# A decoder layer in float32 by split products: first units, phase borders and the last coupling factors rearranged

## The reference

```
combined = 0.7 * gf + 0.3 * coupling_net(out)        # 512 -> 512 -> 256 -> 128 -> 1, gelu, sigmoid
coupling = 0.1 + adaptive_range * (combined - 0.5) * 2.0
out = out + coupling * twist(out)                    # twist permutes the four channel quarters, with signs
```

## Time and profile before

| | us |
|---|---|
| median of 3 runs | 2162.09 (2159.74 to 2171.07) |
| profiled execution, its own time | 2165.26 |
| its span | 2163.2 |
| PE busy, share of span | 1814.4, 84% |
| DVE busy | 1488.3, 69% |
| ACT busy | 1256.2, 58% |
| POOL busy | 857.7, 40% |

### The profile page before, as it was taken

One profiled execution on the slowest core, in us unless ns is written; L12 is line 12 of the kernel. 1 busy time (PEld: TensorE's weight loads), 2 busy tenths in 40 slices (PEclk: granted clock), 3 DMA queues, 4 the chain that ended last, 5 costly groups with the idle time before them and its releaser, 6 DMA issues. The chain is left out here.

```text
span 2163.2 us, 29349 instructions
## 1 busy us (share of the span) xinstructions
PE 1814.4 (84%) x8616; PEld 1353.1 (63%) x8616; DVE 1488.3 (69%) x2913; ACT 1256.2 (58%) x2664; POOL 857.7 (40%) x774
## 2 busy tenths in 40 slices
PE   6588888888888888888875999999958999988873
PEld 5465655656566565665434888888846777776652
DVE  6667677676776767677535666666644788888776
ACT  3277777777867868777752222222224677666754
POOL 4467767676775857768501222222210000000000
PEclk9689999999999999999887999999978999999986
DMA  4132132222323123132215111111031111212111
GB/s 143 37 91 59 49 98 58 88 58 62 88 54 108 46 77 86 34 98 59 80 37 180 59 58 58 58 58 58 20 103 58 59 54 45 78 59 78 59 39 58
DMA packets 90197, 148.90 MB, mean 69 GB/s; under 512 B 16496, under 2 KB 19568, under 8 KB 90096
## 3 DMA queue, kind: packets, MB, share of 16 engines
q1 hardware_dynamic: 90096, 147.76, 22.3%
HBM read 63.82 MB, written 33.55 MB: 45 GB/s over the span
## 5 line engine op out<-in xcount | busy, mean ns | idle before, releaser
L479 DVE TENSOR_REDUCE a_neg_max<-a_max 128x1 fp32r<-128x512 f32 x512 | 342.0, 687 | 175.5 <-PE a_max L819 170.0
L713 ACT ACTIVATE a_probs<-a_exp 128x512 f32<-128x512 f32 x512 | 294.2, 605 | 206.8 <-PE a_exp L837 205.9
L692 ACT ACTIVATE a_max<-a_max,a_neg_max 128x512 f32<-128x512 f32 x512 | 346.9, 689 | 27.0 <-DVE a_neg_max L479 26.5
L819 PE MATMUL a_max<-a_stack 96*128 96x512 f32 x512 | 223.5, 461 | 101.6 <-ACT a_max L692 90.7
L819 PEld LDWEIGHTS a_max<-a_stack 96*128 96x128 f32 x512 | 100.3, 199 | 195.9 <-ACT a_max L692 156.4
L837 PE MATMUL a_exp<-a_stack 100*128 100x512 f32 x512 | 197.7, 427 | 25.2 <-ACT a_probs L713 21.9
L794 PE MATMUL a_t<-a_w_hi,a_zT_hi 128*128 128x384 f32 x512 | 187.8, 367 | 26.3 <-DVE a_v L444 13.3
L317 POOL TENSOR_TENSOR a_rstd<-a_rstd,a_minus_half 128x16 f32<-128x16 f32 x64 | 186.2, 2909 | 44.4 <-DVE a_rstd L463 41.6
L795 PE MATMUL a_t<-a_w_lo,a_zT_hi 128*128 128x384 f32 x512 | 181.7, 355 | 0.0
L796 PE MATMUL a_t<-a_w_hi,a_zT_lo 128*128 128x384 f32 x512 | 181.2, 354 | 0.0
L1158 POOL TENSOR_TENSOR r_part<-r_part 128x512 f32<-128x512 f32 x32 | 45.8, 1431 | 315.1 <-DVE r_part L1205 315.1
(11 more groups left out here) (249 smaller groups left out, 4884.5 us busy)
## 6 DMA issues: line engine op xcount, KB each, us to landing
a_stack<-a_nT_hi SPq DMA_DIRECT2D x512, 64.0 KB, 2.0
a_stack<-a_nT_lo SPq DMA_DIRECT2D x256, 64.0 KB, 2.0
a_z<-x SPq DMA_DIRECT2D x8, 1024.0 KB, 7.3
a_y<-x SPq DMA_DIRECT2D x8, 1024.0 KB, 5.4
x<-a_y SPq DMA_DIRECT2D x8, 1024.0 KB, 4.2
r_xn<-x SPq DMA_DIRECT2D x8, 1024.0 KB, 5.6
r_cn<-ctx SPq DMA_DIRECT2D x8, 1024.0 KB, 7.8
x<-r_xn SPq DMA_DIRECT2D x8, 1024.0 KB, 4.3
```

The source lines that it names most:

```text
L479: nc.vector.tensor_reduce(neg_max[:, t, ROW + h:ROW + h + 1].bitcast(F32R), bank_max[i % NB][:, :], AX_X, ALU.max, negate=True).then_inc(m ...
L692: nc.scalar.activation(bank_max[i % NB][:, :], bank_max[i % NB][:, :], ACT.Exp, bias=neg_max[:, t, ROW + h:ROW + h + 1], accum_out=sums[:, ...
L713: nc.scalar.activation(probs[:, kt % 2, h, :], bank_exp[i % 2][:, :], ACT.Exp).then_inc(exp_done, 1)
L819: mm(bank_max[i % NB][:, :], stack[0:ROW, par, h, t * P:(t + 1) * P], stack[0:ROW, par, HG + h, :], start=True, stop=True).then_inc(score_ ...
```

## The change

Four places change.

- First units. `x_stats` of sequence 1 stands between unit 0's two `head_mean`, its fourth tile ahead of `turn_low(0, 0)`, `x_final` ahead of `turn_low(0, 1)`. Unit 2's projection gets four banks of its own and stands ahead of all query scores: two tiles behind the transposition of unit 0's first side, one behind the second side, the last behind `nTlo_done` 1. All `save_qkv` of unit 2 stand ahead of `row_max`. SP regroups units 0 and 1 side by side (key side of all four heads first), each as soon as its side is there. The head statistics `head_var(1, 1)` stay behind the fourth `row_max`.
- First border. Retention's weights, x1 and context of its first batch are loaded within attention once all projections are done, into the dead `w_hi`, `w_lo`; they are split into dead buffers, four of six parts (1024 columns each) in slots 3, 5, 8, 10 of the last unit, two around the last additions; DVE also takes the statistics and normalises x there (`next_stats` in slot 2, `next_norm` in slot 9). PE does 36 of the 48 output projections in slots 3 to 14 of the last unit. x1 is stored in four parts. The `turns` and `decay` tables are still loaded in retention, now first.
- Second border. Batch 7 follows a list of its own, `R_LAST`, with entries for coupling: `c_stats` and `c_shift` (DVE, POOL), `c_norm` (ACT), `c_split` 0 to 8 (ACT high, DVE low). Its loads are issued once the last v is projected. Coupling starts with the transpositions.
- Coupling. The third cycle's coupling is not multiplied in on 512 columns: PE turns `coupling`, `alpha` and `beta` (12 transpositions in place of 8) and DVE multiplies on 4 columns (`take_scale`, 8 small instructions in place of 3). `sums`, `l3_out`, `y`, `y_moments`, `y_norm` and `normalise` 3 move in `STAGES`.

```diff
+            def regroup_side(U, par, s):
+                c = SIDES[s]
+                sp.wait_ge(nTlo_done, 2 * U + s + 1)
...
-            regroup(0, 0)
-            regroup(1, 1)
+            for U in range(2):
+                for s in range(2):
+                    regroup_side(U, U, s)
...
-            sp.wait_ge(y_sum, T * B)
-            sp.dma_start(rows(x1, B - 1), y[:, :, :]).then_inc(x1_out, 16)
-            sp.wait_ge(x1_out, 16 * B)
+            sp.wait_ge(qkv_done, T * G * B)
+            for m in (0, 2, 1):
+                sp.dma_start(ret.raw[m], w_next[("Wk", "Wq", "Wv")[m]].rearrange("(k p) n -> p k n", p=P)).then_inc(ret.load_w, 16)
+            sp.dma_start(ret.xn[:, 0], rows(x1, 0)).then_inc(ret.x_in[0], 16)
+            sp.dma_start(ret.cn[:, :, :], rows(ctx_in, 0)).then_inc(ret.c_in, 16)
+            for t in range(T):
+                sp.wait_ge(y_sum, T * (B - 1) + t + 1)
+                sp.dma_start(x1[B - 1, t * P:(t + 1) * P, :], y[:, t, :]).then_inc(x1_out, 16)
+            sp.wait_ge(x1_out, 16 * (B - 1) + 16 * T)
...
+            def next_lower(m, half):
+                raw, hi, lo = ret.split_part(m, half)
+                dve.wait_ge(ret.w_high, SPLITS.index((m, half)) + 1)
+                nc.vector.tensor_tensor(lo, raw, hi.bitcast(F32), ALU.subtract).then_inc(ret.w_low, 1)
...
+                    if left == 0 and i == R_STATS_AT:
+                        next_stats()
+                    if left == 0 and i == R_NORM_AT:
+                        next_norm()
+                    if left == 0 and i in SPLIT_AT:
+                        next_lower(*SPLITS[SPLIT_AT.index(i)])
...
-            for s in range(2):
-                head_mean(0, s)
+            head_mean(0, 0)
+            for t in range(3):
+                x_stats(1, t)
+            head_mean(0, 1)
...
+            x_stats(1, 3)
             turn_low(0, 0, bank_t[0])
             rotate(1, 0)
             head_mean(1, 0)
+            x_final(1)
...
-            for h in range(HG):
-                for t in range(T):
-                    row_max(0, T * h + t)
-                if h == 0:
+            for t in range(T):
+                save_qkv(2, 2, t, bank_2[t])
+            for i in range(T * HG):
+                row_max(0, i)
+                if i == 3:
                     head_var(1, 1, False)
-                save_qkv(2, 2, h, bank_t[h % 2])
-                x_stats(1, h)
-            x_final(1)
...
             attn_low(G * B - 1, G - 1)
+            next_lower(*SPLITS[-2])
             for t in range(T):
-                add_out(B - 1, t, bank_t[t % 2])
+                add_out(B - 1, t, bank_last[t])
+            next_lower(*SPLITS[-1])
...
+                    if left == 0 and OUT_PART_AT <= i < OUT_PART_AT + T * (G - 1):
+                        if i == OUT_PART_AT:
+                            pe.wait_ge(attnT_done, U)
+                            pe.wait_ge(summed, T * HG * (U + 1))
+                            pe.wait_ge(maxrow_saved, 2 * (U + 1))
+                            pe.wait_ge(nTlo_done, 2 * (U + 1))
+                        project_out_part(*divmod(i - OUT_PART_AT, G - 1))
...
+            pe.wait_ge(qkv_saved, T + 3)
+            turn_heads(0, 0, bank_t[0])
+            for t in range(3):
+                if t == 2:
+                    pe.wait_ge(qkv_saved, T + 4)
+                    turn_heads(0, 1, bank_t[1])
                 for k in range(K):
-                    project(2, 2, h, k, bank_t[h % 2])
+                    project(2, 2, t, k, bank_2[t])
+            pe.wait_ge(nTlo_done, 1)
+            for k in range(K):
+                project(2, 2, 3, k, bank_2[3])
+            for i in range(T * HG):
+                query_scores(0, 0, i)
...
-            pe.wait_ge(nTlo_done, 2 * G * B)
-            pe.wait_ge(inverse_saved, G * B)
             for t in range(T):
-                if t >= 2:
-                    pe.wait_ge(y_sum, T * (B - 1) + t - 1)
-                project_out(B - 1, t, bank_t[t % 2])
+                project_out_part(t, G - 1)
...
+R_LAST = [(name, arg) for name, age, arg in R_STAGES if age == "now"][:19] + [
+    ("scores", 0), ("v_out", 3), ("scores", 1), ("mask", 0), ("mask", 1), ("c_stats", 0), ("scores", 2), ("s_out", 0),
+    ("mask", 2), ("c_split", 0), ("s_out", 1), ("c_split", 1), ("scores", 3), ("c_shift", 0), ("s_out", 2),
+    ("c_split", 2), ("mask", 3), ("c_split", 3), ("weigh", 0), ("s_out", 3), ("weigh", 1), ("c_norm", 0), ("c_norm", 1),
+    ("add", 0), ("c_split", 4), ("c_norm", 2), ("c_norm", 3), ("add", 1), ("weigh", 2), ("c_split", 5), ("weigh", 3),
+    ("add", 2), ("c_split", 6), ("c_split", 7), ("c_split", 8), ("add", 3)]
...
+            sp.wait_ge(v_done, T * B)
+            sp.dma_start(cou.xn[:, :, :], rows(x2, 0)).then_inc(cou.x_in, 16)
...
+            for dst, src in loads_w:
+                sp.dma_start(dst, src).then_inc(cou.load, 16)
...
+            for dst, src in loads_small:
+                sp.dma_start(dst, src).then_inc(cou.load_small, 16)
             store(B - 1, 1)
+            sp.wait_ge(cou.load_small, 16 * len(loads_small))
...
+                dve.wait_ge(cou.split_high, i + 1)
+                nc.vector.scalar_tensor_tensor(lo, raw, sign, hi.bitcast(F32), ALU.mult, ALU.subtract).then_inc(cou.split_low, 1)
...
+                act.wait_ge(cou.load, 16 * 4)
+                nc.scalar.activation(hi, raw, ACT.Copy, scale=sign).then_inc(cou.split_high, 1)
...
-    ("first", "new", 0), ("l3", "run", 0), ("scale", "old", 0), ("first_out", "new", 0), ("first_low", "new", 0),
-    ("first", "new", 1), ("y_scale", "old", 0), ("y", "old", 0), ("l3_out", "run", 0), ("z", "run", 0),
+    ("first", "new", 0), ("l3", "run", 0), ("scale", "old", 0), ("first_out", "new", 0), ("l3_out", "run", 0),
+    ("first_low", "new", 0), ("first", "new", 1), ("y_scale", "old", 0), ("y", "old", 0), ("z", "run", 0),
...
-    ("normalise", "next", 3), ("mul", "run", (2, 3)), ("mix", "run", (2, 3)), ("mixed", "run", (2, 1)),
+    ("mul", "run", (2, 3)), ("mix", "run", (2, 3)), ("mixed", "run", (2, 1)),
...
-    ("mixed", "run", (2, 3)), ("l2", "run", (2, 3)), ("second_out", "new", 3), ("y", "old", 2), ("y", "old", 3),
-    ("y_moments", "old", 0), ("transpose", "next", 0), ("transpose", "next", 1), ("transpose", "next", 2),
-    ("l2_out", "run", 2), ("turned", "next", 0), ("l3", "run", 2), ("turned", "next", 1), ("y_shift", "old", 0),
-    ("l3_out", "run", 2), ("l2", "new", (0, 0)), ("l2", "new", (0, 1)), ("z", "run", 2), ("transpose", "next", 3),
-    ("turned", "next", 2), ("y_norm", "old", 0), ("turned", "next", 3), ("sums", "run", 0), ("couple", "run", 2),
-    ("l2", "new", (0, 2)), ("l2", "new", (0, 3)), ("l2_out", "new", 0), ("gate", "new", 2)]
+    ("mixed", "run", (2, 3)), ("l2", "run", (2, 3)), ("sums", "run", 0), ("second_out", "new", 3),
+    ("normalise", "next", 3), ("y", "old", 2),
+    ("transpose", "next", 0), ("transpose", "next", 1), ("transpose", "next", 2), ("l2_out", "run", 2), ("y", "old", 3),
+    ("l3", "run", 2), ("y_moments", "old", 0), ("l3_out", "run", 2), ("turned", "next", 0), ("turned", "next", 1),
+    ("y_shift", "old", 0), ("l2", "new", (0, 0)), ("l2", "new", (0, 1)), ("z", "run", 2), ("transpose", "next", 3),
+    ("turned", "next", 2), ("y_norm", "old", 0), ("y_norm", "old", 1), ("turned", "next", 3), ("tanh", "run", 2),
+    ("l2", "new", (0, 2)), ("l2", "new", (0, 3)), ("l2_out", "new", 0), ("gate", "new", 2),
+    ("y_norm", "old", 2), ("y_norm", "old", 3)]
+
...
-                nc.vector.tensor_tensor(part[:, :], coupling[:, :], beta[:, :], ALU.mult).then_inc(dve_step, 1)
...
-                nc.vector.tensor_tensor(coupling[:, :], coupling[:, :], alpha[:, :], ALU.mult).then_inc(dve_step, 1)
...
-                nc.vector.tensor_tensor(alpha[:, :], alpha[:, :], part[:, :], ALU.subtract)
-                nc.vector.tensor_tensor(beta[:, :], beta[:, :], coupling[:, :], ALU.add).then_inc(coupled, 1)
...
+                nc.vector.tensor_copy(turned_rows[:, :, :], by_token[:, :, :, 0]).then_inc(scale_done, 1)
+                dve.wait_ge(scale_done, b + 1)
+                third, first, second = (turned_rows[:, i, :] for i in range(3))
+                nc.vector.tensor_scalar(third, third, derived[:, 2:3], base[:, par:par + 1], ALU.mult, ALU.add).then_inc(dve_step, 1)
...
+                nc.vector.tensor_tensor(crossed[:, 0, :], third, second, ALU.mult)
+                nc.vector.tensor_tensor(crossed[:, 1, :], third, first, ALU.mult).then_inc(dve_step, 1)
+                dve.wait_ge(dve_step, steps.next())
+                nc.vector.scalar_tensor_tensor(scale[:, 0, :], crossed[:, 0, :], -1.0, first, ALU.mult, ALU.add).then_inc(dve_step, 1)
+                nc.vector.tensor_tensor(scale[:, 1, :], second, crossed[:, 1, :], ALU.add)
+                nc.vector.scalar_tensor_tensor(scale[:, 2, :], second, -1.0, crossed[:, 1, :], ALU.mult, ALU.subtract)
+                dve.wait_ge(dve_step, steps.next())
```

(7 more changed lines are left out.)

414 lines of the change are left out of this document (235 added, 179 removed).

## The result

The changed kernel takes 2097.91 us (median of 4 runs, 2091.10 to 2099.41), the kernel before beside it 2164.32 us (median of 4, 2159.74 to 2171.07): ratio 0.9684, interval 0.9659 to 0.9710. The profiled execution took 2096.84 us with a span of 2093.9 us, against 2165.3 and 2163.2. So 66 us by the medians and 69.3 us by the spans, where 79 were forecast; 2097.91 lies inside 2060 to 2110.

A forecast was written before the change was run, and what follows sets the result against it. It took PE, with DVE close behind, to bound coupling passes, and chains of transfers and small steps the start and borders. Terms -13 - 24 - 14 - 28 = -79 us gave 2083 us, range 2060 to 2110.

The forecast's parts named there:

- First units: Start of attention: projections and statistics moved into existing waits bring the loop's start earlier, -13 us (from -8 to -17).
- First border: Attention to retention: 20.8 us in place of 44.9 up to retention's first product, -24 us (from -15 to -28).
- Second border: Retention to coupling: last addition +7.4 us, first coupling product at 1618.8 instead of 1632.76, -14 us (from -8 to -18).
- Coupling: Coupling passes, their boundaries and the end: PE's waits go or shrink, -28 us (from -15 to -50).
- pass 8 and the end: End of coupling: waits of 2.3 and 1.5 us into and in pass 8 go, and 1.8 us net at the end.
- rival 3: Start of attention: POOL's rotation or unit 1's stack holds the loop, -2 in place of -13, 2094 us; chance 7%.
- The longer unit: Attention's last unit, with 36 output projections moved in, ends 3.3 us later; bounds 0 and +12 (low clock throughout).
- Rival 1: Whole kernel: thin cover, last unit at the low clock, smaller gains at every place, -52 us, 2110; chance 17%.
- ACT's wait for the four loads: Second border: ACT's first weight split waits until 1593.5 for all four weights, holding later steps; last addition +7.4 us.
- Steady passes: Coupling: a pass becomes 57.3 us from 61.0 (bounds -1.5 and -8); six such boundaries give -22.2 us.
- Rival 2: Coupling: PE's wait and the low clock behind it both go, a pass is 53.0 us, total 2057.5; chance 15%.
- Rival 4: Coupling: the new order lengthens the chain between passes, +7.7 us a pass in place of -3.7, total 2173; chance 2%.

## Why the prediction was right, and where it was off

Forecast and traced executions, step by step:

| step | forecast | traced |
|---|---|---|
| start of attention's loop | -13 | 107.10 to 94.53: -12.6 |
| the loop to the last unit | 0 | 995.6 to 998.8: +3.2 |
| the last unit, longer | +3.3 | 15.9 to 19.1: +3.2 |
| from there to retention's first product | -27.4 | 44.9 to 16.1: -28.8 |
| to the last v product | 0 | 418.4 to 416.2: -2.2 |
| last addition, later | +7.4 | 15.7 to 25.3: +9.6 |
| last addition to first coupling product | -21.4 | 34.4 to 12.2: -22.1 |
| seven passes, six boundaries | -22.2 | 450.9 to 429.2: -21.7 |
| pass 8 and the end | -5.6 | 79.5 to 81.6: +2.1 |
| sum | -79 | -69.3 |

**First units.** Right, to half a microsecond; undoing them gave 12.0 us back. On the way the second `head_mean` of unit 0 came 2.2 us later (42.07 to 44.28), where 1.5 were forecast. What holds the loop's start is POOL's rotation, as the forecast had it; rival 3 (-2) is out.

**First border.** Right in each of its terms to within 1 us: 3.9 us to the end of the last addition (4.5), 2.6 to the next block (3.5), 0.7 for the identity and 8.9 to the first product (8.8). The longer unit was the one bold step (3.3 us against bounds of 0 and 12); the experiment without the products shows 2.5 us in the unit for 7.6 behind it. Rival 1's thin cover did not come.

**Second border.** The block change and what follows came out at 12.2 us (forecast 13.0), the last addition 9.6 us later in its batch (7.4). The forecast put the delay to ACT's wait for the four loads. That wait was there (7.37 us), but taking it away gave only 3.1 us of 9.6. The larger part lies, by the rows, with DVE's added work, which the forecast named and did not price by itself; that part is argued and not shown.

**Steady passes.** 57.9 us (57.3). The six passes gave 2.9 to 4.3 us each, 20.6 in all; the first pass, in which nothing was forecast, gave the other 1.1 (81.7 us, and the same with coupling's part undone, so it is not the new order). The wait ahead of `l3` is gone, one near 2 us stands ahead of `l2` of cycle 1, and 1.0 us ahead of the first product (0.8). Rival 2 (53 us) did not come: the clock falls behind the new wait as it did behind the old one, for 3 us or so, and the waits themselves are longer than its 0.6 us. Its price of the clock is real: where the new wait became 1.42 us the clock was 1.00, PE was busy 51.9 us (its 52.4) and a pass took 56.2 us. Rival 4 (68.7 us) is out. The Trainium skill (TensorE: Matmul & The Clock Gate, section HAM oscillation — how this bites in real kernels) tells of a kernel whose array fell to the low clock after its wait for data in every single round. The rows agree where the wait was 2.58 us; they do not in every pass where it was 2.1, and with coupling's part undone one pass (58.9 us) kept the clock at 1.00 behind a wait of 3.65 us:

```profile
1799.79 0.47 PE L2047 MATMUL f_l<-f_h_hi,f_w_hi 128*128 128x512 f32 x1 [3.65 <-DVE f_h_lo L1768]
```

**The step that failed** is the last of Coupling: "The one into pass 8 waits 2.3 us, another of its waits gives 1.5 us. At the end PE's wait of 4.47 us for the last product gives 1.8 us". Where 5.6 us of gain were forecast there were 2.1 us of loss. The wait into pass 8 did go (z of its cycle 0 was 2.4 us ahead), and the path from the last z to the factors was 1.5 us shorter. Two things took this back, and more.

The first is the store of y, a term that the forecast put at nothing. The change issues it later: in pass 8 by the split of `y_norm`, which puts it behind the normalisation of tiles 2 and 3, at the end mainly by the later places of y 2, y 3, `y_moments` and `y_shift`. The forecast counted the split as two `y_norm` less ahead of `turned` 3 and did not ask who waits for the store. It is ACT, with the next batch's scaling in the same buffer: 2.8 and 4.3 us of wait, of which DVE feels 2.1 and 2.9. In the steady passes ACT waits 1.4 us, of which DVE feels 0.3. Halves of y take 7.0 us back, but only 3.4 of them in this step.

The second is DVE's order in pass 8. Since z of cycle 0 comes sooner, y 0 and y 1, which DVE had done or begun ahead of it, now stand between it and `beta`. From that z to `beta` it is 2.4 us in the kernel before, 5.6 in the changed one, and still 3.6 with the store's wait gone:

```profile
2098.50 0.55 DVE L1725 TENSOR_SCALAR f_beta<-f_coupling,f_derived,f_base 128x512 f32<-128x512 f32 x1 [0.68 <-ACT f_coupling L1882]
...
2025.57 0.53 DVE L1886 TENSOR_SCALAR f_beta<-f_coupling,f_small,f_base 128x512 f32<-128x512 f32 x1
```

The rows are of the kernel before (z at 2096.09) and of the run with y in halves (z at 2022.01). So the forecast's other wait of 1.5 us was not won: that stretch is 1.0 us longer than before even with the halves, and pass 8 with the end gives 1.3 us and not 5.6. (The rest of the difference is 0.9 us behind products at the low clock in the cycle after it, and 0.9 at the end, where ACT still waits 1.79 us for a half.) That coupling with the halves comes to 26.5 us, near the 28 of the forecast, is therefore luck: the steady passes give more than forecast and this step less.

**The rest of the distance.** The spans miss the forecast by 9.7 us: 7.7 in this step, 3.2 in attention's loop (chance, as the second trace of before shows), the others within 2.2 each and of both signs. Another 5 us lie between execution and median: the forecast took 3.2 us off for it, the execution after was 1.1 us under its own median, and its time fell by 0.9 us less than its span.

What stays open: retention's 2.2 us. Its products of the weights with the turned inputs, into `r_even` and `r_odd`, take 0.227 us a step in place of 0.233, which over 768 of them would be near 5 us. Operands and order are the same, their places in SBUF are not; no run moved these alone, and what takes the rest back is open too.
